# The second cross attention's value and output projections: moved into the attention block, the output projection in three passes

## The reference

```
q = (layernorm(x) @ w_q) as 16 heads of 64
k, v = (ctx @ w_k), (ctx @ w_v) as 16 heads of 64
attn = softmax(q k^T / 8)          # per head, 64 x 1024
out = (attn v), heads side by side # 64 x 1024
x = x + out @ w_o
```

## Time and profile before

| | |
|---|---|
| median of 3 runs | 1034.07 us (1034.07, 1031.37, 1034.31) |
| profiled execution, its own time | 1030.17 us |
| span of its instructions | 1027.4 us |
| PE busy, weight loads busy | 973.0, 805.2 us |
| DVE, ACT, POOL busy | 554.1, 494.3, 163.8 us |
| mean granted TensorE clock | 0.983 |

### The profile page before, as it was taken

One profiled execution on the slowest core, in us unless ns is written; L12 is line 12 of the kernel. 1 busy time (PEld: TensorE's weight loads), 2 busy tenths in 40 slices (PEclk: granted clock), 3 DMA queues, 4 the chain that ended last, 5 costly groups with the idle time before them and its releaser, 6 DMA issues. The chain is left out here.

```text
span 1027.4 us, 21006 instructions
## 1 busy us (share of the span) xinstructions
PE 973.0 (95%) x8776; PEld 805.2 (78%) x8776; DVE 554.1 (54%) x804; ACT 494.3 (48%) x708; POOL 163.8 (16%) x170
## 2 busy tenths in 40 slices
PE   8899999888799989899999999999999989979997
PEld 7688888665689975699999999999989976547554
DVE  4578777666444444665656564646565621386222
ACT  4677776353666635544454545444454420313221
POOL 2000000022134413012121211111111100420000
PEclk9999999899999999999999999999999999998999
DMA  5122110022023313111111111111130000999990
GB/s 152 45 66 64 46 49 3 9 56 64 26 77 93 92 46 119 42 42 41 42 42 41 41 41 41 41 41 41 41 122 0 1 1 1 268 338 291 285 300 20
DMA packets 55205, 81.40 MB, mean 79 GB/s; under 512 B 5201, under 2 KB 44578, under 8 KB 55138
## 3 DMA queue, kind: packets, MB, share of 16 engines
q1 hardware_dynamic: 55138, 80.43, 25.9%
HBM read 79.89 MB, written 0.52 MB: 78 GB/s over the span
## 5 line engine op out<-in xcount | busy, mean ns | idle before, releaser
L186 PE MATMUL ps<-f_pT_hi,f_cN_hi 128*128 128x256 f32 x512 | 145.4, 284 | 2.4 <-DVE f_pT_lo L1778 2.4
L186 PE MATMUL ps<-f_pT_hi,f_cN_lo 128*128 128x256 f32 x512 | 144.7, 283 | 0.0
L186 PE MATMUL ps<-f_pT_lo,f_cN_hi 128*128 128x256 f32 x512 | 144.7, 283 | 0.0
L1525 ACT ACTIVATE e_pr<-ps,e_negmax 128x1024 f32<-128x1024 f32 x64 | 71.5, 1117 | 129.8 <-DVE e_negmax L1530 127.6
L1778 DVE TENSOR_TENSOR f_pT_lo<-ps,f_pT_hi 128x1024 fp32r<-128x1024 f32 x64 | 78.3, 1223 | 82.1 <-ACT f_pT_hi L1726 82.1
L1726 ACT CAST f_pT_hi<-ps 128x1024 fp32r<-128x1024 f32 x64 | 65.0, 1015 | 84.9 <-PE ps L1815 84.8
L186 PE MATMUL ps<-e_cT_hi,e_qb_hi 128*128 128x512 f32 x256 | 105.6, 413 | 0.0
L409 DVE SCALAR_TENSOR_TENSOR a_u<-ps,a_floor,a_cap 128x1024 f32<-128x1024 f32 x64 | 79.2, 1280 | 45.9 <-PE ps L490 45.9
L186 PEld LDWEIGHTS ps<-f_pT_hi,f_cN_hi 128*128 128x128 f32 x512 | 97.8, 191 | 4.4 <-DVE f_pT_lo L1778 2.6
L186 PE MATMUL ps<-e_cT_hi,e_qb_lo 128*128 128x512 f32 x256 | 100.7, 393 | 0.0
L186 PE MATMUL ps<-e_cT_lo,e_qb_hi 128*128 128x512 f32 x256 | 99.8, 390 | 0.0
(11 more groups left out here) (379 smaller groups left out, 1990.4 us busy)
## 6 DMA issues: line engine op xcount, KB each, us to landing
k_w<-in_L_ffn_W SPq DMA_DIRECT2D x30, 1024.0 KB, 14.5
a_ctxT<-in_ctxT SPq DMA_DIRECT2D x16, 512.0 KB, 3.7
d_w<-in_L_ffn_w SPq DMA_DIRECT2D x32, 256.0 KB, 2.8
e_rawT<-in_ctxT SPq DMA_DIRECT2D x8, 1024.0 KB, 5.0
e_raw<-in_ctx SPq DMA_DIRECT2D x8, 1024.0 KB, 5.7
k_b<-in_L_ffn_b SPq DMA_DIRECT2D x14, 256.0 KB, 12.1
e_wq<-in_L_xattn_w_q SPq DMA_DIRECT2D x1, 1024.0 KB, 5.1
e_wk<-in_L_xattn_w_k SPq DMA_DIRECT2D x1, 1024.0 KB, 7.7
```

The lines of the kernel that those rows point to most:

```text
L186: last = nc.tensor.matmul(out, a[i], b[j], start=start and n == 0, stop=stop and n == 2, skip_group_check=skip)
L1525: nc.scalar.activation(pr[:, p % NPR, :], core.ps[p % 2][:], ACT.Exp, bias=negmax[:, p:p + 1], accum_out=total[:, p:p + 1]).then_inc(exp_r ...
```

## The change

The block `g_` is gone; its work stands in the block `f_`.

- PE: in the last batch, `values(0)` and `values(1)` (the two pairs' products with `wv`, as before) stand between the last transposes and `outputs(b, 3, 0)`, `values(2)` and `values(3)` after the last `outputs`. Then follow pairs 0 and 1 of the output projection for all four row blocks, `values(4)` and `values(5)`, pairs 2 and 3, `values(6)` and `values(7)`, pairs 4 and 5, and at the end pairs 6 and 7 row block by row block, with a signal after each. Each product of the output projection is now `product3`: 96 passes in place of 32 full-precision products. Each row block has a bank of its own (4 to 7), since all four accumulate at once.
- The halves of a projected pair (`o2`) lie in the buffers of the queries' halves (`e_qb_hi`, `e_qb_lo`), four slots; the halves of `wo` (`wo2`) lie in those of the context's features (`e_cT_hi`, `e_cT_lo`).
- ACT: `outputs` of group 2, then the high half of `wo`, `attended(0)` (pair 0's high half), `outputs` of group 3, `attended(1)` to `attended(7)`. POOL makes the low half of `wo`, DVE each pair's low half.
- DVE adds to `x` one row block at a time and takes the statistics of each behind its addition. The norm of the next block begins at `bn_aggr` (`first=TT`).
- PE runs 5 unread products at the block's end and 10 in place of 16 at the next block's start.
- `e_rawT` and `e_raw` are one buffer, with the same two parts.

```diff
-        self.vector_stats(step, src)
+        self.vector_stats(step, src, first)
...
-        for j in range(TT):
+        for j in range(first, TT):
             step(nc.vector.bn_stats(c.stats[:, j, :], src[:, j, :]), j == TT - 1)
...
+            o2 = [q[:].rearrange("p c n -> p (c n)").rearrange("p (r n) -> p r n", n=NT) for q in qb]
+            wo2 = [t[:].rearrange("p c s -> p (c s)").rearrange("p (h d) -> p h d", d=D) for t in cT]
...
 gpsimd, at the end:
+                pool.wait_ge(wo_hi, 1)
+                nc.gpsimd.tensor_tensor(wo2[1], wo[:], wo2[0].bitcast(F32), ALU.subtract).then_inc(wo_lo, 1)
...
 scalar:
+                def attended(p):
+                    act.wait_ge(v_psum, p + 1)
+                    nc.scalar.copy(o2[0][:, p % 4, :], core.bank(p % 4)).then_inc(oT_act, 1)
...
+                    else:
+                        act.wait_ge(v_in, 32)
+                        nc.scalar.copy(wo2[0], wo[:]).then_inc(wo_hi, 1)
+                        attended(0)
                     outputs(b, 3)
...
+                for p in range(1, HP):
+                    attended(p)
...
 vector, at the end:
+                for p in range(HP):
+                    dve.wait_ge(oT_act, p + 1)
+                    nc.vector.tensor_tensor(o2[1][:, p % 4, :], core.bank(p % 4), o2[0][:, p % 4, :].bitcast(F32), ALU.subtract
+                                            ).then_inc(oT_dve, 1)
+                for j in range(TT + 1):
+                    if j < TT:
+                        dve.wait_ge(y_psum, j + 1)
+                        nc.vector.tensor_tensor(x[:, j, :], x[:, j, :], core.bank(4 + j)[:, 0:D], ALU.add
+                                                ).then_inc(x_out, 1)
+                    if j >= 1:
+                        dve.wait_ge(x_out, j)
+                        nc.vector.bn_stats(core.stats[:, j - 1, :], x[:, j - 1, :]).then_inc(x_stats, 1)
+                dve.wait_ge(x_stats, TT)
...
 tensor:
+                def values(p):
+                    if p >= 4:
+                        pe.wait_ge(oT_dve, p - 3)
+                    pe.wait_ge(o_read, NG * (B - 1) + p // 2 + 1)
...
+                def project(p, j):
+                    cols = slice(j * P, j * P + P)
+                    return product3(nc, core.bank(4 + j)[:, 0:D], [o[:, p % 4, cols] for o in o2],
+                                    [w[:, p, :] for w in wo2], p == 0, p == HP - 1)
...
                     transposes(b, HP - 1)
                     if more:
                         pe_scores(pe, b + 1, 0)
+                    else:
+                        pe.wait_ge(v_in, 32)
+                        pe.wait_ge(exp_ready, HP * B)
+                        values(0)
+                        values(1)
                     outputs(b, 3, 0)
...
+                values(2)
+                values(3)
+                pe.wait_ge(pT_lo, HP * B)
+                pe.wait_ge(o_read, NG * B)
+                pe.wait_ge(wo_lo, 1)
+                for p in range(0, HP - 2, 2):
+                    pe.wait_ge(oT_dve, p + 2)
+                    for j in range(TT):
+                        project(p, j)
+                    for j in range(TT):
+                        project(p + 1, j)
+                    if p + 4 < HP:
+                        values(p + 4)
+                        values(p + 5)
+                pe.wait_ge(oT_dve, HP)
+                for j in range(TT):
+                    project(HP - 2, j)
+                    project(HP - 1, j).then_inc(y_psum, 1)
+                core.warm(0, 5)
...
 next block:
-            norm.vector(dve, step)
+            norm.vector(dve, step, TT)
...
-            norm.tensor(pe, 16)
+            norm.tensor(pe, 10)
```

More of the change, by code:

```diff
@@ L117, in __init__, with vector_stats @@
         self.xnT = core.sem(tag + "_xnT_ready")
-    def vector_stats(self, step, src):
+    def vector_stats(self, step, src, first=0):
         c, nc = self.c, self.c.nc
-        for j in range(TT):
+        for j in range(first, TT):
             step(nc.vector.bn_stats(c.stats[:, j, :], src[:, j, :]), j == TT - 1)
@@ L124, in vector_stats, with vector_norm @@
             step(nc.vector.bn_aggr(c.meanvar[:, j, :], c.stats[:, j, :]), j == TT - 1)
-    def vector_norm(self, eng, step, src, dst, eps, ready):
+    def vector_norm(self, eng, step, src, dst, eps, ready, first=0):
         c, nc = self.c, self.c.nc
-        self.vector_stats(step, src)
+        self.vector_stats(step, src, first)
         nc.vector.tensor_scalar(c.vareps[:], c.meanvar[:, :, 1], eps, None, ALU.add).then_inc(self.var, 1)
@@ L142, in vector_rstd, with vector @@
         step(nc.vector.scalar_tensor_tensor(c.rstd[:], c.newton[:], 1.5, c.rstd[:], ALU.add, ALU.mult))
-    def vector(self, eng, step):
+    def vector(self, eng, step, first=0):
         c, nc = self.c, self.c.nc
-        self.vector_norm(eng, step, c.x, c.xn, LN_EPS, self.xn)
+        self.vector_norm(eng, step, c.x, c.xn, LN_EPS, self.xn, first)
         self.vector_transposed(eng)
@@ L1476, in xattn1 @@
         qc = core.sb("e_qc", [P, DC, B, H * T], F32, ctx)
-        rawT, raw = core.sb("e_rawT", [P, DC, S], F32, ctx), core.sb("e_raw", [P, KT, D], F32, ctx)
+        both = core.sb("e_raw", [P, DC * S + KT * D], F32, ctx)
+        rawT = both[:, 0:DC * S].rearrange("p (c s) -> p c s", s=S)
+        raw = both[:, DC * S:DC * S + KT * D].rearrange("p (k d) -> p k d", d=D)
         cT = [core.sb("e_cT_" + n, [P, DC, S], F32R, ctx) for n in ("hi", "lo")]
@@ L1674, in xattn1 @@
                                                      sem("o_read"))
+            o2 = [q[:].rearrange("p c n -> p (c n)").rearrange("p (r n) -> p r n", n=NT) for q in qb]
+            wo2 = [t[:].rearrange("p c s -> p (c s)").rearrange("p (h d) -> p h d", d=D) for t in cT]
+            v_psum, oT_act, oT_dve = sem("v_psum"), sem("oT_act"), sem("oT_dve")
+            wo_hi, wo_lo = sem("wo_hi"), sem("wo_lo")
+            y_psum, x_out, x_stats = sem("y_psum"), sem("x_out"), sem("x_stats")
             block = inner.enter_context(nc.Block())
@@ L1828, in outputs @@
                     last.then_inc(o_psum, 1)
+                def values(p):
+                    if p >= 4:
+                        pe.wait_ge(oT_dve, p - 3)
+                    pe.wait_ge(o_read, NG * (B - 1) + p // 2 + 1)
+                    for g in range(2):
+                        h = 2 * p + g
+                        for c in range(DC):
+                            last = nc.tensor.matmul(core.bank(p % 4)[HD * g:HD * g + HD, :],
+                                                    wv[:, c, h * HD:(h + 1) * HD],
+                                                    qc[:, c, :, h * T:(h + 1) * T], start=c == 0, stop=c == DC - 1)
+                    last.then_inc(v_psum, 1)
+                def project(p, j):
+                    cols = slice(j * P, j * P + P)
+                    return product3(nc, core.bank(4 + j)[:, 0:D], [o[:, p % 4, cols] for o in o2],
+                                    [w[:, p, :] for w in wo2], p == 0, p == HP - 1)
                 def batch(b):
```

## The result

The changed kernel takes 1027.38 us (median of 6 runs, 1022.58 to 1028.44) against 1034.05 for the kernel before (6 runs), a ratio of 0.9945 with the interval 0.9922 to 0.9967. Measured again beside other kernels, the same program came to 0.9929 (0.9906 to 0.9952). The two ratios are worth 5.7 and 7.3 us, and neither interval holds 1, so it is faster, by little; 1026.1 was forecast. One of the 24 executions of the kernel before in that second measurement took 1318.22 us at a mean clock of 0.689 and is left out of its ratio.

A forecast was written before the change was run, and what follows sets the result against it. TensorE, busy 973.0 of 1027.4 us, was taken as the bound. 6.40 us from the block's end plus 0.80 from the next norm made 7.20, from 1033.3 to 1026.1 us; 8-in-10 range 1022.0 to 1030.5.

The forecast's parts named there:

- the restarts: PE's seven changes between full-precision and three-pass products at the block's end: taken as 0 us, upper end 0.8.
- the tail: Behind PE's last pass: 0.16 us later end, 0.93 for addition, one `bn_stats` and signals, 0.32 for the barrier.
- the norm: Next stage's norm without its four `bn_stats`: 0.80 of 1.40 us gained, the square-root table load being late next.
- the stretch of 39.4 us: End of second cross attention, from issue of the last transposes to DVE beginning the next stage: 39.36 us becomes 32.96.
- The waits of the block's end: The 1.10 us for ACT's last copy and the barrier, and PE's 0.87 wait for the last pair's copy, both go.
- The wait filled: Value products of pairs 0 and 1 fill PE's 2.46 us wait before the last weighted sums; the gap is gone.
- Three passes: Output projection as 96 passes at 0.1217 us, 11.68 in place of 14.08 for 32 full-precision products: 2.40 less.
- rival D: Weight loads not hidden in the output projection: 313 ns a pass, 18.3 us more, 1044.4 us; chance 3%.
- Halves in time: Rounded halves ready before PE's output projection wants them: 1.2 us cover for pairs, 4.0 for `wo`; no path cost.
- B: Rival: a half of a pair or of `wo` comes late for the output projection, about 1027.3 us; chance 8%.
- C: Rival: PE still waits before value products of pairs 0 and 1, up to 2.4 us return, 1028.5; chance 5%.
- Rival A: Half-clock stretches near the kernel's end fall over busy expert work: gain 3 to 6 us, 1027 to 1030.5; chance 20%.

The follow-up runs named there:

- run by fours: Changed kernel with value products and output-projection passes taken by four pairs, not two: ratio 0.9938 (0.9917 to 0.9958) to the kernel before.
- all four edits: Changed kernel with pairs by four, GpSimd's last constants late, statistics back in the norm, no unread products at the end, warm-up 14: ratio 0.9919 to before.
- by four, constants late: Changed kernel with pairs taken by four, GpSimd's last constants behind the norm's last output, warm-up 12: ratio 0.9937 (0.9911 to 0.9962) to before.

## Why the prediction was right

**Direction and size.** 7.20 us were summed. From the last transposes to the first projection the profiles show 46.51 - 40.94 = 5.57, repeated in both pairs of profiles. That is 1.63 less than forecast: 0.95 in the restarts, 0.40 in the tail, 0.28 in the norm, each below. The medians differ by 6.67; the rest is within the scatter with the clock. With 5.57 from the measured 1034.05 the sum would have given 1028.5, so part of the closeness of 1026.1 to 1027.38 is luck.

**Its own signs.** The prediction called itself wrong if the stretch of 39.4 us didn't become 32 to 34. It became 34.31 (35.24 less the 0.93 from the transposes' start to where that stretch began), outside by 0.3. The next stage starts 5.05 us earlier for 6.4, the groups of value products take 3.63 for 3.5, the 96 passes 11.99 for 11.7, and the square root comes at 1.26 for 1.3. The mechanism stood and its size was a fifth too large.

**The waits of the block's end: gone, but not tested apart.** The 1.10 for the border and the 0.87 before the last pair's copy were to go, and in the changed profile PE is busy without a gap there. No run puts them back alone.

**The wait filled: right.** 2.24 of the 2.41 between the gap's 2.46 and the 0.05 start.

**Three passes: right in size, the rival D refuted.** 2.34 for 2.40. Loads of 191 ns run beside matmuls 0.12 us apart here too. So the rule in the section "Part 3: Packing small matmuls" of the Trainium skill's "TensorE: Matmul & The Clock Gate", by which loads overlap only when the row group differs, doesn't describe these loads.

**Halves in time: right.** PE never waits for `e_qb_lo` or `wo`'s low half: pair 1's low half is done at 847.53 and wanted at 849.26. B didn't occur, nor did C.

**"Restarts" was the mis-sized term.** I took 0 with an end at 0.8, "since with no wait there is no restart". The first unread product came at +33.43, not +32.48: 0.95 more for seven changes, above the upper end too. The run by fours showed that they cost this without any wait. The whole cost is larger. Within a group one value product follows the other by 0.43 us and one pass the other by 0.12, which makes 31.04 for the 32 and 144 of them; the stretches of the changed profile add up to 32.46. That is 1.42, 0.20 a change. The prices 0.437 and 0.1217 were means over whole stretches, with their ends in them, and so held 0.46 of it already.

**The tail: 0.40 short.** The distance from the last pass's successor to the next stage is 1.81; I had 1.41. Of this 0.22 is the barrier behind DVE's wait for its statistics (0.54 for 0.32; without the statistics it is 0.32 again), the rest the second statistics operation behind the last addition, where I had counted one.

**The norm: 0.52 for 0.80.** The root came at +1.26 from the stage's start, as said. But in the kernel before one select of GpSimd hit one DVE operation (0.62 for 0.16, at 875.26), and in the changed one, where the square root comes 0.80 earlier, two were hit, for 0.73 us in place of 0.46. With the selects out of the way the term is as predicted: from the stage's start to the projection are 5.76 us with the statistics (all four edits) and 4.96 without them (by four, constants late), 0.80 apart.

**Rival A happened at another place.** In this profile the two stretches over the router stayed within 0.4 us of where they were in time, and the program came to them only 1.2 us earlier. In the other ten profiles of changed kernels the first starts between 912 and 922 us, and the second lasts 3.4 us in six of them, in place of 6.8. A new one, 875.6 to 879.0 us, fell over the first projections in this profile and cost 1.5 us; in the second profile of the same program it was absent. One reading was off: the stretch at 920.4 did not follow the idle time of 5.35 us but began inside it, as PE was idle from 917.11 to 922.46.

**The base.** I took 1033.3 for the unchanged kernel, between its median and mean. Over all measurements its median was 1030.5 to 1034.1, so the choice was good to 3 us and no better.

## What to carry to other kernels

Fill a wait of PE with work that stands later anyway, and take it in few, long groups: each change between these value products (64 output columns) and the passes cost about 0.2 us though nothing waited. When a step is moved ahead of a barrier, price what it adds to the last engine's tail there; moving the statistics gained 0.52 behind the barrier (0.80 with GpSimd's selects out of the way) and lost 0.87 before it. And compare profiles from a common point: here the same code reached it up to 6 us apart.

## What the runs showed of the hardware

- DVE is held up by GpSimd's selects: 0.16 became 0.52, 1.38 became 1.76 us, each until a select of 0.62 had ended, and both were gone when the selects came later. Not every operation is held: DVE's copy of `xnT` out of PSUM took 0.69 us beside such a select (by four, constants late) and without one. Beside memsets of GpSimd nothing was held up by more than 0.07 us (`vareps`, 0.24 for 0.17), and whether a memset did that is not shown. For the operations on `newton` and `rstd` this agrees with the Trainium skill, "SBUF — State Buffer", section "Who interferes with whom": a DVE instruction with two SBUF inputs contends with a GpSimd instruction that reads SBUF, not with one that only writes. `xn` has one tensor as input and two columns of one value per row, and of these that sentence says nothing.
- A group of value products (64 output columns) takes 0.19 us more than 0.43 for each product, with eight of them (3.63) as with sixteen (7.07), and whether full-precision products or passes stood beside them. The first pass behind a group adds 0.11 and the first value product behind passes 0.09. From the last pass to the unread products (128 output columns, full precision) the distance is 0.12, as between passes, so neither the change of precision nor that from 256 moving columns to 128 costs anything there. Which property of the value products does was not tried.
- The granted clock differed between executions of one program: 0.973 to 0.985 on average, 1034.5 to 1028.7 us. In the profiles the difference lay at several places: near 280 and 380 us some show 10.2 us at half clock and others 3.4, and the two profiles of the kernel before, alike there, come to the same product at 214.25 and 216.78 us.
